# Sliding the small tensors of a LoRA feed-forward kernel so that every on-chip tensor starts at a multiple of 128 bytes

## The reference, cut to what matters

```python
gate = lora_add(einsum('bnh,fh->bnf', x, W_gate), x, A_gate, B_gate)   # rank 16, scale 0.5, by index
up   = lora_add(einsum('bnh,fh->bnf', x, W_up),   x, A_up,   B_up)
act  = silu(gate) * up
down = lora_add(einsum('bnf,hf->bnh', act, W_down), act, A_down, B_down)
x_abs_max = clip(max(abs(down), axis=-1), 1e-5)
out  = einsum('bsd,od->bso', down / x_abs_max, QUANT_LEVELS[weight_2bit])
return x + (out * (x_abs_max * weight_scale) + bias)
```

## Time and profile before

| what | value |
|---|---|
| median of 3 runs | 935.93 us (935.86, 935.93, 937.17) |
| profiled execution, its own time | 936.85 us |
| its span, first to last instruction | 934.9 us |
| TensorE matmul busy | 904.2 us, 97% of the span |
| VectorE, ScalarE, GpSimd busy | 352.0, 259.4, 80.3 us |
| mean granted TensorE clock | 0.991 |
| DMA | 45.38 MB, 49 GB/s over the span |

### The profile page before, as it was taken

The page is one execution under the profiler, slowest core; times in us unless marked ns, Lnnn a source line. Parts: engine busy times, 40 slices in busy tenths (PEclk is TensorE's granted clock), DMA queues, the critical chain, the costliest instruction groups (busy, mean ns, idle before and its releaser), DMA issues.

```text
span 934.9 us, 13664 instructions
## 1 busy us (share of the span) xinstructions
PE 904.2 (97%) x3930; PEld 718.4 (77%) x3930; DVE 352.0 (38%) x754; ACT 259.4 (28%) x448; POOL 80.3 (9%) x110
## 2 busy tenths in 40 slices
PE   2999999999999999999999999999999999999995
PEld 2777777777777777877777777777777777777873
DVE  3563345222542234422353224432255223543224
ACT  2442243111522124211242213421142212422112
POOL 0011003000030000300003100121003000200200
PEclk9899999999999999999999999999999999999998
DMA  3655121111112011020111102111111111111001
GB/s 96 154 164 160 39 57 32 43 34 29 43 40 54 22 35 51 26 66 11 49 48 34 45 12 55 54 34 34 29 48 45 46 31 32 57 26 31 12 14 49
DMA packets 45445, 45.38 MB, mean 49 GB/s; under 512 B 13168, under 2 KB 31984, under 8 KB 45392
## 3 DMA queue, kind: packets, MB, share of 16 engines
q1 hardware_dynamic: 43024, 41.85, 16.5%
q10 hardware_dynamic: 2368, 3.02, 1.2%
HBM read 36.44 MB, written 8.39 MB: 48 GB/s over the span
## 4 chain that ended last, share of the span: by engine, by line
PE 95%; DVE 1%; SPq 1%; ACT 1%; DMA 1%; issue 0%; DVEq 0%
PE pw_up L1702 26%; PE pw_gate L1702 24%; PE pw_down L1746 24%; PE ps_misc L1771 6%; PE pw_td L1735 4%; PE ps_misc L1702 2%; PE pw_down L1756 2%; PE pw_up L1712 2%; PE pw_gate L1712 2%; PE ps_misc L1763 1%; DMA plan_room<-places 0%; SPq L304 0%; SPq L316 0%; PE pw_down L1702 0%; DVE amax L1366 0%
## 5 line engine op out<-in xcount | busy, mean ns | idle before, releaser
L1746 PE MATMUL pw_down<-wd,wact_split 128*128 128x512 f32 x960 | 237.0, 396 | 0.0
L1702 PE MATMUL pw_up<-wxs,wgu 128*128 128x512 f32 x948 | 233.2, 395 | 0.0
L1746 PEld LDWEIGHTS pw_down<-wd,wact_split 128*128 128x128 f32 x960 | 180.8, 188 | 47.5
L1702 PE MATMUL pw_gate<-wxs,wgu 128*128 128x512 f32 x864 | 215.7, 399 | 0.1
L1702 PEld LDWEIGHTS pw_up<-wxs,wgu 128*128 128x128 f32 x948 | 178.7, 188 | 41.8
L1702 PEld LDWEIGHTS pw_gate<-wxs,wgu 128*128 128x128 f32 x864 | 160.4, 188 | 36.7 <-issue 0.5
L1352 DVE TENSOR_TENSOR wact_full<-pw_up,wact_full 128x512 f32<-128x512 f32 (+1 forms) x87 | 60.0, 690 | 311.6 <-PE pw_up L1712 307.1
L991 ACT ACTIVATE wact_full<-pw_gate 128x512 f32<-128x512 f32 (+1 forms) x80 | 47.8, 597 | 286.5 <-PE pw_gate L1712 286.5
L1003 ACT ACTIVATE wact_split<-wact_full 128x512 fp32r<-128x512 f32 x80 | 50.5, 631 | 70.1 <-DVE wact_full L1352 70.1
L1357 DVE TENSOR_TENSOR wact_split<-wact_full,wact_split 128x512 fp32r<-128x512 f32 x80 | 55.4, 693 | 26.2 <-ACT wact_split L1003 26.0
L1771 PE MATMUL ps_misc<-wq,wdt_split 128*128 128x512 f32 x224 | 56.9, 396 | 0.0
(11 more groups left out here) (119 smaller groups left out, 671.6 us busy)
## 6 DMA issues: line engine op xcount, KB each, us to landing
out<-rows SPq DMA_DIRECT2D x120, 64.0 KB, 1.6
rows<-x_tok SPq DMA_DIRECT2D x112, 64.0 KB, 1.8
rows<-w_gu SPq DMA_DIRECT2D x8, 512.0 KB, 4.1
x_raw<-x_feat SPq DMA_DIRECT2D x60, 64.0 KB, 1.8
x_more<-x_feat SPq DMA_DIRECT2D x60, 64.0 KB, 1.8
wb_raw<-b_rows SPq DMA_DIRECT2D x32, 92.0 KB, 2.8
low_room<-b_rows SPq DMA_DIRECT2D x32, 80.0 KB, 2.5
rows<-w_down SPq DMA_DIRECT2D x9, 256.0 KB, 3.8
```

Of the source, the lines that this page charges most:

```text
L1702: last = nc.tensor.matmul(bank, w, wxs[:, xp, k, :], start=(n == 0 and k == 0), stop=False, skip_group_check=(f == 0))
L1746: last = nc.tensor.matmul(pw_down[:, s, :], wact(ap, f)[:, s * P:(s + 1) * P], wd[:, wp, f, :], start=(f == 1 and n == 0), stop=False)
```

## The change: one tensor for the scales, a padded plan

The five small tensors become column ranges of one tensor `scales` of 32 floats (128 bytes), and `plan` grows from 73 to 96 integers (384 bytes). The instructions, their order, their waits and their DMAs stay as they are. `scales` starts at 162944, `plan` at 163072, and the room behind it at 163456, a multiple of 128. All that lay behind `plan` moves up by 32 bytes, and as the sizes of those tensors are multiples of 128, each of them then leaves 0. The tensors ahead of `scales` stay where they are.

```diff
-        wscale = sb("wscale", [P, 1])
-        ones = sb("ones", [P, 1])
-        amax = sb("amax", [P, WSUBS])
-        rinv = sb("rinv", [P, WSUBS])
-        ascale = sb("ascale", [P, WSUBS])
-        plan = sb("plan", [P, BATCH // 2 + WTILES + 1], I32)
+
+        scales = sb("scales", [P, 32])
+        wscale = scales[:, 0:1]
+        ones = scales[:, 1:2]
+        amax = scales[:, 4:4 + WSUBS]
+        rinv = scales[:, 8:8 + WSUBS]
+        ascale = scales[:, 12:12 + WSUBS]
+        plan = sb("plan", [P, 96], I32)
```

## The result

The change makes the kernel 1% faster: 927.38 us as the median of four runs (926.57 to 929.12) against 936.36 for the kernel before beside it. The ratio is 0.9901, with a 95% interval of 0.9889 to 0.9912. I had forecast no change, 936.0 us, with 933.6 as the lower end of the range.

A forecast was written before the change was run, and what follows sets the result against it. TensorE was taken to bound the kernel, busy 904.2 of 934.9 us. The sum was 936.85 + 0 + 0 + 0 + 0 = 936.85, taken as 936.0 for a median of like runs; range 933.6 to 938.4 us.

The forecast's parts named there:

- I take 0 for TensorE: All matmuls: the address move changes their pace by 0, within 0.5 ns each, 1.5 us either side over 2996 matmuls.
- nearest row: Warm-up matmuls, both operands from wgu, 256 columns, shortest 277 ns: taken to show an aligned pair no faster, 0.461 ns a column.
- the 19 ns: 512-column matmuls: some 19 ns of each 232.5 are not columns, the place where an address could matter.
- The first rival: TensorE matmuls: two aligned operands run faster; 879 us at full price, 930 at 2 ns a matmul; chance 0.12.
- The second rival: TensorE matmuls: weight load and moving reads starting at the same place within 128 bytes meet, slower, 943.5 us; chance 0.10.
- The 235 ns: Line 1735, operands in step: two matmuls in 0.47 us, 235 ns each, cited for the slower rival against 232.5 at line 1702.
- The third rival: Kernel start: plan landing and first matmuls shift against the clock's rise, 1.0 us either way, 935.0 to 937.0; within no change's 0.78.
- ScalarE and VectorE at 0: Their work beside TensorE costs nothing; on the path only in the first and last 20 us, 0 with 0.4 us either side.
- the 20 ns to `x_raw`: ScalarE: 1063 ns from aligned x_raw against 1043 from x_more; line 957 from x_more may read 1063 after the change.
- DMA at 0: Landings in plan_room and x_more on the path: no change, bound 0.5 us either side; later loop landings are covered.
- `plan` and the scales at 0: Queue reads of plan and 16 short VectorE operations on scales: cost 0; even 10 ns each would be 0.2 us.
- The page cited: Engine reads have a grain of 16-byte cachelines; 96 and 0 are both multiples, so no engine would see the move.

The follow-up runs named there:

- matmuls alone: Kernel of float32r matmuls only, 24 to a line, operand starts varied, run once; 227 ns each at line 57 (both on multiples of 1024), 237.5 with the moving one 4 bytes further.
- the padded plan: Kernel before with the five scale tensors left apart and plan padded to 88 integers, large tensors addressed as in the kernel after; 927.02 us, ratio 0.9900.

## Why the prediction was wrong, point by point

**The step that failed** is the first of the sum: "I take 0 for TensorE", with 0.5 ns to either side. The times of 512 columns that it rests on were read right, but for the wrong variable. I sorted the pairs by who is on a boundary of 128 and saw no difference; the variable was the distance modulo 256, and in the kernel before no pair of 128 weight columns and 512 moving ones was at distance 0. `wxs` less `wgu` was 224, `wd` less `wact_split` and `wq` less `wdt_split` 160, line 1712 128. All were slow alike, and I read that as insensitive. The rows at distance 0 were half of line 1735's (the even chunks) and the warm-up, and the runs showed that 32 and 64 weight columns and 256 moving ones don't have the effect. So the "nearest row", from which I argued, could not have shown it. Its subtraction was unsound besides: it took the 277 ns of a pair in step from the 395 of pairs out of step, and called the 0.461 ns a column the aligned pair's. With both in step (matmuls alone, lines 96 and 57) the mean durations are 284 and 389 ns, 0.41 a column.

The bound was no bound. I had named the 19 ns beside the columns as the place where an address could act, and then bounded the unknown case by the spread of the known ones. The rows admitted -6 ns as well as 0: the unknown case was the one that the change makes. In place of 0 the runs showed 6.6 ns for each matmul that has settled in step, and, settling included, 1.1 us a tile for the 264 matmuls against `wgu` and `wgu_first`, some 9 us over the eight tiles.

**The first rival** (two aligned operands run faster; 0.12) had the sign and the place right (its mark was 2.75 us or less for 12, and `pw_up` has 2.73), and the condition wrong: both aligned to 128 is neither needed (wgu and wxs both at 96: 928.57 us) nor enough (128 apart: 935.18). Its size lay between the two I gave, 6 ns for 264 matmuls a tile, less what settling costs. **The second rival** (operands in step meet, slower) had the right variable, their distance, though modulo 128, and the wrong sign. The 235 ns that it took from line 1735 are a rounding of hundredths: over the five tiles that line takes 231.8.

**The third rival** (the start, 1.0 us either way) holds for the first matmul against `wgu_first`, at 24.73 us before and 24.54 after. Its bound was too small for what follows: tile 0 takes 99.1 us in the execution profiled after, where TensorE waits 1.3 us at 49.9 us for ScalarE, and 97.7 us with a wait of 0.5 in the one with the padded plan, whose large tensors lie at the same addresses. That is a spread between executions, and none of it is in the period of a tile.

**ScalarE and VectorE at 0**: held. From `x_more`, now on a boundary:

```profile
L959 ACT ACTIVATE wxs<-x_more x8: 1044/1047/1056, 23.4 to 785.0; 128x1024 fp32r<-128x1024 f32 x8
...
DMA to landing us min/median/max: 1.6/1.8/3.7
```

1047 ns after 1043, not 1063: the 20 ns to `x_raw` are not the address's phase. **DMA at 0**: held for the medians, which stay 1.8 us, and for the landing on the path in `plan_room`, which went from 4.08 to 3.93 us. The longest landing in `x_more` rose from 3.1 to 3.7, 0.1 beyond my bound, and is not on the chain of the first 36 us. **`plan` and the scales at 0**: held, and shown by the padded plan alone.

**The page cited** on cachelines of 16 bytes (the Trainium skill, "SBUF — State Buffer", section "Door 1: The DMA port swizzle") speaks of successive accesses of one operand and has no grain under which 96 and 0 differ. It says nothing of two operands; the measurement decides, and by it the starts of two operands matter together up to 256 bytes.

## What to carry to other kernels

Where an engine is the bound and its instruction takes longer than its arithmetic, ask what that remainder hangs on before calling an edit free; a row bounds an unseen case only if it has the same shape. For float32r matmuls of 128 weight columns and 512 moving ones, give the two operands' tensors starts that are equal modulo 256 bytes (unused padding does it): 3% on the matmul, 1.6% on this kernel. Nothing here promises that for other shapes: at 496 columns it was 0.4%, and at 256 in step was the slower. When a rule such as "everything on a multiple of 128" helps, test a version that obeys it and should fail, and one that breaks it and should work.

## What was not expected of the hardware

The bf16 matmul of 512 columns takes 215.8 ns, what the Trainium skill has for a warm clock ("TensorE: Matmul & The Clock Gate", section "Wait — 56ns, not 53.3ns?", 215.7). A float32r one takes 226.7 at best and 233.3 mostly, which no row here explains. Nor does any explain why the gap between the two paces all but goes at 496 columns, why 64 bytes of distance give 228.9 where 32 and 96 give 233.3, why 4 bytes are the worst (237.5), and why some matmuls behind a change of shape are slower before the pace settles. That the weights' read and the moving read meet in one memory is a guess; that short weights don't gain speaks against its simplest form, and it stays open. Open too is whose weights count, those of the matmul itself or those of the next one, loaded meanwhile: in every line of these kernels all stationary operands have the same phase, so no line tells the two apart.
